# Reading the second half's two banks of maxima in one VectorE instruction, with a new order of TensorE's matmuls

## The reference

```python
scores = jnp.einsum('bhqd,bhkd->bhqk', Q, K) / (TAU * np.sqrt(hd).astype(np.float32))
A = jax.nn.softmax(scores, axis=-1)
...
A_stable = LAMBDA_JUMP * A + (1.0 - LAMBDA_JUMP) * L[None, None, :, :]
out = jnp.einsum('bhqk,bhkd->bhqd', A_stable, V)
```

## Time and profile before

| | |
|---|---|
| median of 3 runs | 1935.2 us (1935.0 to 1937.52) |
| the profiled execution | 1934.62 us |
| its span | 1932.8 us |
| mean granted TensorE clock | 0.995 of 2.4 GHz |
| TensorE busy | 1889.9 us, 98% of the span |
| VectorE busy | 1629.0 us, 84% |
| ScalarE busy | 1299.1 us, 67% |
| line 677, reads of maxima | 2048, from 79.2 to 1324.7 us |

### The profile page before, as it was taken

The page is one execution under the profiler, slowest core; times in us unless marked ns, Lnnn a source line. Parts: engine busy times, 40 slices in busy tenths (PEclk is TensorE's granted clock), DMA queues, the critical chain, the costliest instruction groups (busy, mean ns, idle before and its releaser), DMA issues. The chain is left out here.

```text
span 1932.8 us, 41897 instructions
## 1 busy us (share of the span) xinstructions
PE 1889.9 (98%) x16092; PEld 1116.2 (58%) x16092; DVE 1629.0 (84%) x3147; ACT 1299.1 (67%) x2390; POOL 372.0 (19%) x380
## 2 busy tenths in 40 slices
PE   7999999999999999999999999999998999999997
PEld 3554444444444444444444444444586899999997
DVE  6799999999999999999999999994277755555554
ACT  3348888888888888888888888888544422322232
POOL 1362110010101110101010101011045622223233
PEclk9999999999999999999999999999999999999999
DMA  7954456645564556455645454543246777878884
GB/s 258 260 111 90 89 113 111 107 90 112 109 109 90 112 106 112 89 114 101 113 92 114 100 111 95 104 100 82 91 139 209 286 226 221 257 253 256 288 255 113
DMA packets 132021, 279.65 MB, mean 145 GB/s; under 512 B 41696, under 2 KB 72416, under 8 KB 125152
## 3 DMA queue, kind: packets, MB, share of 16 engines
q1 hardware_dynamic: 118672, 259.17, 53.6%
q0 software_dynamic: 13152, 17.83, 4.7%
HBM read 215.93 MB, written 79.06 MB: 153 GB/s over the span
## 5 line engine op out<-in xcount | busy, mean ns | idle before, releaser
L677 DVE TENSOR_REDUCE part_max<-psum 128x1 f32<-128x512 f32 x2048 | 1232.8, 676 | 4.3 <-PE psum L782 3.0
L738 ACT ACTIVATE probs<-psum 128x512 f32<-128x512 f32 x2048 | 1064.4, 601 | 169.2 <-PE psum L791 162.8
L782 PE MATMUL psum<-max_k,max_q 48*128 48x512 f32 x2048 | 696.1, 459 | 0.1
L791 PE MATMUL psum<-score_q,score_k 50*128 50x512 f32 x2048 | 629.8, 428 | 0.8 <-issue 0.6
L803 PE MATMUL psum<-probs,v_ones 128*32 128x256 f32 x8192 | 601.6, 388 | 6.4 <-ACT heads_sb L744 6.3
L782 PEld LDWEIGHTS psum<-max_k,max_q 48*128 48x128 f32 x2048 | 316.6, 183 | 224.1 <-DVE part_max L677 205.3
L791 PEld LDWEIGHTS psum<-score_q,score_k 50*128 50x128 f32 x2048 | 320.2, 184 | 198.4 <-ACT probs L738 146.3
L803 PEld LDWEIGHTS psum<-probs,v_ones 128*32 128x32 f32 x8192 | 188.1, 108 | 257.6 <-issue 146.0
L1236 ACT ACTIVATE x_sb<-psum,x_sb 128x512 f32<-128x512 f32 (+1 forms) x160 | 101.7, 636 | 260.0 <-PE psum L1607 257.8
L1626 PE MATMUL psum<-w,h_hi 128*128 128x256 f32 x1120 | 208.5, 282 | 0.1
L1626 PEld LDWEIGHTS psum<-w,h_hi 128*128 128x128 f32 x1120 | 181.0, 188 | 10.8 <-DVE h_lo L1426 0.3
(11 more groups left out here) (177 smaller groups left out, 1242.5 us busy)
## 6 DMA issues: line engine op xcount, KB each, us to landing
w<-w_split SPq DMA_DIRECT2D x40, 2048.0 KB, 8.5
max_q<-qk_pieces SPq DMA_DIRECT2D x192, 128.0 KB, 6.9
score_k<-qk_pieces SPq DMA_DIRECT2D x192, 128.0 KB, 4.6
xs<-in_pads SPq DMA_DIRECT2D x33, 528.0 KB, 4.6
qk_pieces<-pieces SPq DMA_DIRECT2D x32, 512.0 KB, 4.7
w_split<-w_pair SPq DMA_DIRECT2D x32, 512.0 KB, 5.3
max_k<-qk_pieces SPq DMA_DIRECT2D x192, 64.0 KB, 7.1
score_q<-qk_pieces SPq DMA_DIRECT2D x192, 64.0 KB, 2.3
```

The lines of the kernel that those rows point to most:

```text
L677: nc.vector.tensor_reduce(part_max[:, u, t, q:q + 1], ps_m[q // 2][:, 1 - q % 2, :], axis=AXIS.X, op=ALU.max).then_inc(m_read, 1)
L738: nc.scalar.activation(probs[:, kb % PROBS, chunk * BLOCK:(chunk + 1) * BLOCK], bank_of(k, kb, c), ACT.Exp, scale=float(HD) ** -0.5).then_ ...
L782: nc.tensor.matmul(ps_m[p][:, h, :], max_q[u][rows, t * P:(t + 1) * P], max_k[u][rows, p * BLOCK:(p + 1) * BLOCK], start=True, stop=True). ...
L791: nc.tensor.matmul(bank_of(k, kb, c), score_k[u][rows, kb * P:(kb + 1) * P], score_q[u][rows, part * BLOCK:(part + 1) * BLOCK], start=True ...
```

## The change

In `maxima`, VectorE reads the first pair of banks one by one as before, and the second pair with one instruction over 128 x 1024 elements that waits for both matmuls. It counts `m_read` three times a tile in place of four, so `part_max` has three columns a tile, and the waits on `m_read` are rewritten: the matmuls of q = 2 and q = 3 both wait for the one read of the second pair. The loop over two tiles has a new order of the same calls. (S is a score, M a maximum, V a value.)

Before: S M S M V M M S S S M V V M S S M S M V

After: S M M S V S S M M S M V V S M S S M M V

```diff
+READS = 3
...
-            for q in range(4):
-                if q == 2 and between is not None:
-                    between()
+            for q in range(2):
                 dve.wait_ge(m_ready, 4 * g + q + 1)
-                nc.vector.tensor_reduce(part_max[:, u, t, q:q + 1], ps_m[q // 2][:, 1 - q % 2, :],
+                nc.vector.tensor_reduce(part_max[:, u, t, q:q + 1], ps_m[0][:, 1 - q, :],
                                         axis=AXIS.X, op=ALU.max).then_inc(m_read, 1)
+            if between is not None:
+                between()
+            dve.wait_ge(m_ready, 4 * g + 4)
+            nc.vector.tensor_reduce(part_max[:, u, t, 2:3], ps_m[1].rearrange("p b f -> p (b f)"),
+                                    axis=AXIS.X, op=ALU.max).then_inc(m_read, 1)
 
         def split_shift(m, u):
 
-            dve.wait_ge(m_read, 4 * ST * (m + 1))
+            dve.wait_ge(m_read, READS * ST * (m + 1))
...
             if g > 0:
-                pe.wait_ge(m_read, 4 * g + q - 3)
+                pe.wait_ge(m_read, READS * (g - 1) + min(q + 1, READS))
...
-                pe.wait_ge(m_read, 4 * ST * NHEADS)
+                pe.wait_ge(m_read, READS * ST * NHEADS)
...
         for _ in range(NHEADS * ST // 2):
             score()
             maximum()
+            maximum()
+            score()
+            value()
+            score()
             score()
             maximum()
-            value()
             maximum()
-            maximum()
-            score()
-            score()
             score()
             maximum()
             value()
             value()
+            score()
             maximum()
             score()
             score()
             maximum()
-            score()
             maximum()
             value()
...
-                for n, shape, dt in (("part_max", [P, 2, ST, 4], F32), ("neg_max", [P, ST], F32),
+                for n, shape, dt in (("part_max", [P, 2, ST, READS], F32), ("neg_max", [P, ST], F32),
```

## The result

The changed kernel took 1924.0 us (median of 7 runs, 1919.1 to 1928.6) against 1936.8 us for the kernel before (7 runs, 1935.0 to 1939.2): a ratio of 0.9932, interval 0.9916 to 0.9948. It is faster, by 13 us, where I had forecast 1911 and a range that ended at 1922. The runs also lie further apart than those of before, 9.5 us against 4.2. The profiled execution took 1921.23 us.

What follows compares the result with a forecast made beforehand. VectorE's reads of maxima bound the kernel before; afterwards TensorE, ScalarE and score banks would, in most rounds. 30.7 heads gave -22.4 us and the first 21 tiles 1.4, together -23.8, so 1911 us; range 1900 to 1922, chance 0.85.

Steps and rivals of the forecast that it cites:

- The price of the double read: VectorE's joined read: next read starts 1.13 us behind (1.119 to 1.142), saving 0.066 us a tile.
- TensorE, ScalarE and the score banks as the new bound: Attention loop: scores waiting for exponentials to free banks set rounds of two tiles at 4.68 us, against 4.78 before.
- a first round of 5.22: First two-tile round of a head, held by ScalarE's copy of the last result: 5.22 us, against 5.20 before.
- The waits of weight loads: Sign on TensorE: load waits for maxima down by more than half, those of scores on ScalarE kept or up.
- 4 to 12 forecast: Sign on VectorE: idle before reads, released by TensorE, 4 to 12 us in all, from 2.1 up to 1300 us.
- VectorE as the bound throughout (1901): Rival, attention loop: VectorE still sets the pace, so all 33.8 us are gained, 1901 us; chance 0.24.
- the new order losing the gain: Rival, TensorE's rounds: the new order loses 0.10 us each somewhere unseen, time about 1934 us; chance 0.06.
- S4 late in each round: Rival: a round's fourth score waits for its bank every time, rounds 4.99 us, +52 us, 1987 us; chance 0.07.
- The room that the new order gives: TensorE's maxima behind a double read: VectorE may be 0.3 to 0.4 us late before TensorE feels it.
- the lateness that I had worked out: VectorE's small operations: about 0.49 us late at tile 11 where some 0.38 is free, costing TensorE another 0.11.
- the sum: TensorE's head of 38.01 us plus 0.11 gives 38.12, over 30.7 heads -22.4 us; with the first tiles -23.8.
- rival of a smaller gain: Rival, attention loop: VectorE and TensorE so close that hiccups stop each other; gain 10 to 17 us; chance 0.10.

Runs made afterwards that it cites:

- the first experiment: Changed kernel, but GpSimd splits the next head's shift before scaling, and SyncE sends it before storing the last head: 1912.6 us, ratio 0.9860 to the kernel before.

## Why the prediction was wrong

**The price of the double read: right.** 1.211 us recorded, 1.13 to 1.14 from start to start, in the bounds 1.119 to 1.142. By the Trainium skill's page (VectorE: DVE Perf Modes, the section on the TRN2 errata) a read saved would be worth 0.125 us, as an estimate from its 120 cycles at 0.96 GHz; the traces show 0.06 to 0.07, so the measurement decides.

**TensorE, ScalarE and the score banks as the new bound: right.** Rounds of 4.68 us and a first round of 5.22, heads of 38.12. The waits of weight loads say the same: those of maxima on VectorE fell from 205.3 us to under 9, those of scores on ScalarE rose from 146.3 to 310.3. VectorE waited 17.5 us before double reads, 4 to 12 forecast; 11.6 of them stay when the shift goes first, the rest was the shift. VectorE as the bound throughout (1901) is refuted, as are the new order losing the gain and S4 late in each round.

**The room that the new order gives: wrong, without effect on the time.** I gave the order a part in keeping VectorE's small operations off TensorE. With the old order and the double read heads take the same 38.11 us. The rounds show how (means over heads 1 to 16). With the new order the seventh round of a head, behind the transpose, takes 4.81 us and the others behind the first 4.68: 0.12 us, in the place and nearly the size (0.11) of the lateness that I had worked out. With the old order that round takes 4.71 and the others 4.69 to 4.71. It loses 0.01 to 0.02 in each round and nearly nothing at the transpose, and both come to the same.

**The step that failed** is the sum's "a head takes 38.12, 0.73 less than 38.85", applied to 30.7 heads alike. It put at nothing, without a reason, S3's wait for the next head's shift, a wait that the code shows and that the trace of before shows as met in all heads but 17 and 29. I named the queues in the chain nowhere and did not ask how far ahead of its need the shift came: 1.6 us, of which the change uses up 0.4 to 1.3. The new order takes 0.3 of that by itself (S3 at 34.67 us in place of 34.99), the store in front of the shift most of the rest. With so little left, a store of the shift that takes up to 2.2 us longer stops TensorE for 0.8 to 1.3 us, and a late scaling adds up to 1.0 us by way of the transpose. It cost 9.0 us in the profiled execution and, by the first experiment, some 11 us in the median. With it the sum is -23.8 + 11 = -13, the measured gain. By its number that gain is the prediction's rival of a smaller gain (10 to 17 us), but that one, like the range's upper part, was meant for VectorE and TensorE hindering each other, and this is another cause.

**Still open:** why the number of late heads changes between executions of one program; why the granted clock falls behind some stops of TensorE and not behind others about as long; and why a fetch at 22 us of a head delays the inverse's store by 1 to 2 us more with the fetches moved than at nearly the same place in the changed kernel's early heads. That a fetch packet in front delays small packets is shown by the table and by moving it, though not for every slow store; which engine's ring they share in each head was not followed.

## What to carry to other kernels

When a loop gets shorter, every chain of transfers that was hidden beside it keeps its length. So besides the next engine, list the waits on transfers that are met today, and for each read how long before its need the transfer was issued and how long one takes where it is waited for; if the saving per turn is of the size of what is left, the gain will be given back in part. A new order of the same work counts too, if it moves the instruction that needs the transfer. In a queue worked off in order, what the next turn needs goes in front of what only has to be finished some time. And a wider spread of the runs after a change can be a sign that a chain has lost its slack: here 9.5 us over seven runs, and 1.4 over four once the chain had it back. A stop of TensorE can cost more than its length, so look at the granted clock behind it.

## What the runs showed of the hardware

- The code is a load on the transfer engines. A 16 KB packet of instructions (0.92 us in head 23) that starts 1.0 to 2.5 us behind the issue of the shift's store goes with a median of 4.34 us to the next issue, in place of 2.76, and where it falls depends on the count of instructions ahead: 126 more small instructions in the lead-in made the kernel 24 us slower in the median, 20 of them beyond the lead-in and these in part by the clock, and 252 more gave the old pattern back.
- TensorE's granted clock fell to 1.2 GHz behind some stops of 1.1 to 3.0 us, or in their course: in 5 heads with the fetches moved and in 14 with `LOOK = 22`, for 3.4 to 13.7 us, and a head so hit took up to 46.1 us in place of 38.1.
- Start to start, reads of 512 elements from PSUM stand 0.598 us apart and 1024 elements take 1.13 to 1.14: a fixed part of 0.06 to 0.07 us each is all that joining two of them saves.
